# A routed-expert and time-mix block on one core: a reordered norm head, logit groups of five and three steps, and three row additions moved behind gathers

## Time and profile before

| | |
|---|---|
| Times of three runs, us | 472.74, 472.84, 476.43 |
| Profiled execution, us | 478.51 |
| Its span, us | 476.8 |
| TensorE's granted clock, mean | 0.975 |
| Busy: TensorE, VectorE, ScalarE, GpSimd | 94%, 77%, 50%, 48% |
| Moved by DMA | 77.24 MB |

### The profile page before, as it was taken

How to read it: one execution, slowest core, us unless ns; L and a number is a source line. 1 busy time by engine, 2 the same in 40 slices (tenths; PEclk the granted TensorE clock), 3 DMA queues, 4 the chain that set the end, 5 groups by cost and what they waited for, 6 DMA issues and landing times.

```text
span 476.8 us, 8300 instructions
## 1 busy us (share of the span) xinstructions
PE 445.9 (94%) x2529; PEld 372.7 (78%) x2529; DVE 365.6 (77%) x680; ACT 240.2 (50%) x394; POOL 230.8 (48%) x224
## 2 busy tenths in 40 slices
PE   0897997988999999999999899999999999999997
PEld 0562465877888888888878778888898989898987
DVE  5986596968787898688776589996868787877863
ACT  2784744497586685958565633332414132423131
POOL 5244617616658685679846286742342516070000
PEclk9998758999999999999999999999999999999999
DMA  7999813335764665443463692725343444432001
GB/s 254 393 348 280 218 24 97 93 132 164 268 234 167 214 215 178 121 155 100 144 180 132 240 332 87 242 88 160 121 145 122 127 149 132 154 108 71 24 22 45
DMA packets 45858, 77.24 MB, mean 162 GB/s; under 512 B 5908, under 2 KB 32252, under 8 KB 45820
## 3 DMA queue, kind: packets, MB, share of 16 engines
q1 hardware_dynamic: 37212, 55.83, 33.5%
q0 software_dynamic: 8240, 20.88, 16.6%
q10 hardware_dynamic: 368, 0.04, 0.1%
HBM read 48.52 MB, written 28.21 MB: 161 GB/s over the span
## 4 chain that ended last, share of the span: by engine, by line
PE 69%; DVE 12%; POOL 6%; issue 6%; ACT 4%; DMA 2%; SPq 0%; DVEq 0%; POOLq 0%; ACTq 0%
PE ps_g L1068 13%; PE ps_y L1068 7%; PE ps_w L1528 5%; PE ps_w L1530 5%; PE ps_w L1529 5%; PE ps_w L1595 5%; PE ps_w L1594 5%; PE ps_w L1593 5%; PE ps_G L590 3%; POOL xg L991 3%; PE ps_x L1062 2%; PE ps_h L1088 2%; PE ps_T L578 2%; DMA xT<-x 1%; PE ps_v L1529 1%
## 5 line engine op out<-in xcount | busy, mean ns | idle before, releaser
L991 POOL DMA_INDIRECT xg<-xn_rows,tile_tok x71 | 71.6, 1008 | 32.4 <-issue 17.9
L1504 POOL DMA_INDIRECT yg<-expert_rows,rows x64 | 67.4, 1054 | 23.6 <-issue 17.1
L1068 PE MATMUL ps_g<-w_hi,x_hi 128*128 x142 | 56.6, 398 | 1.8 <-DVE x_lo L1223 1.8
L1068 PE MATMUL ps_g<-w_hi,x_lo 128*128 x142 | 57.0, 401 | 0.0
L1068 PE MATMUL ps_g<-w_lo,x_hi 128*128 x142 | 56.7, 399 | 0.0
L1635 ACT ACTIVATE sact<-ps_w,vec_b 128x512 f32<-128x512 f32 x32 | 22.0, 687 | 58.6 <-PE ps_w L1530 58.6
L1528 PE MATMUL ps_w<-col_hi,s_hi 128*128 128x512 f32 x128 | 50.5, 394 | 0.4 <-DVE shid L1746 0.4
L1530 PE MATMUL ps_w<-col_hi,s_lo 128*128 128x512 f32 x128 | 50.2, 392 | 0.0
L1529 PE MATMUL ps_w<-col_lo,s_hi 128*128 128x512 f32 x128 | 50.2, 392 | 0.0
L1068 PE MATMUL ps_y<-w_hi,h_hi 128*128 x142 | 43.0, 303 | 1.3 <-DVE h_lo L1239 1.3
L1232 DVE TENSOR_TENSOR hid<-ps_g,act 128x512 f32<-128x512 f32 (+1 forms) x36 | 23.7, 658 | 24.4 <-ACT act L1144 24.4
(11 more groups left out here) (245 smaller groups left out, 1276.9 us busy)
## 6 DMA issues: line engine op xcount, KB each, us to landing
expert_rows<-y SPq DMA_DIRECT2D x35, 256.0 KB, 2.2
w_lo<-w_all SPq DMA_DIRECT2D x16, 384.0 KB, 9.1
table<-mix_tables SPq DMA_DIRECT2D x8, 768.0 KB, 6.2
xT<-x SPq DMA_DIRECT2D x16, 256.0 KB, 5.8
xn_rows<-xn SPq DMA_DIRECT2D x16, 256.0 KB, 7.7
xn_columns<-xT SPq DMA_DIRECT2D x8, 512.0 KB, 3.8
col<-xn_columns SPq DMA_DIRECT2D x8, 512.0 KB, 5.0
res<-x SPq DMA_DIRECT2D x16, 256.0 KB, 3.1
```

Of the source, the lines that this page charges most:

```text
L991: pool.indirect_dma_start(out=xg[b][:, t, :], out_offset=None, in_=xn_d[:, :], in_offset=bass.IndirectOffsetOnAxis(ap=tile_tok[:, first_ti ...
L1068: mm = nc.tensor.matmul(out, x[:, k, :], w[:, ds(e, 1), k, cols].rearrange("p o n -> p (o n)"), start=(k == 0 and n == 0), stop=(last and ...
L1504: pool.indirect_dma_start(out=yg[a.buf(2)][:, k, q, :], out_offset=None, in_=y_d[:, :], in_offset=bass.IndirectOffsetOnAxis(ap=picked[a.bu ...
```

## The change

The groups of steps become 0 to 4 and 5 to 7, with strips of 16 partitions; a fifth copy of the bias is loaded. The first two steps of the head are written out in a new order on ScalarE, TensorE and VectorE. TensorE makes all four `less` pieces ahead of the count. VectorE's reciprocal and product of the scores move behind `tile_tok`. GpSimd's `less_first` for pieces 13, 14 and 15 move out of `route` and stand behind the gathers of units 1, 2 and 3.

```diff
-        GROUPS = [(0, 4), (4, NSTEP)]
-        ROWS = P // 4
+        GROUPS = [(0, 5), (5, NSTEP)]
+        ROWS = P // 8
...
-        EARLY = NSTEP // 2
+        EARLY = GROUPS[0][1]
...
-            for i in range(MADE, E * KC):
+            for i in range(MADE, HIGH):
                 less_first(pool, i)
...
-                    act.wait_ge(s_small, 112)
+                    act.wait_ge(s_small, 16 * (EARLY + 3))
...
-            for j in range(4):
+            for j in range(EARLY):
                 act.dma_start(gb[j * ROWS:j * ROWS + E, :], ...)
...
             root(At(0, 0, NSTEP))
-            for i in range(NSTEP):
+            norm(At(0, 0, NSTEP))
+            act.wait_ge(s_const, 8)
+            (ones, before, minus)
+            turned(At(0, 0, NSTEP))
+            root(At(0, 1, NSTEP))
+            norm(At(0, 1, NSTEP))
+            root(At(0, 2, NSTEP))
+            turned(At(0, 1, NSTEP))
+            for i in range(2, NSTEP):
                 if i + 1 < NSTEP:
                     root(At(0, i + 1, NSTEP))
                 norm(At(0, i, NSTEP))
-                if i == 0:
-                    (s_const, ones, before, minus)
-                if i > 0:
+                if i > 2:
                     turned(At(0, i - 1, NSTEP))
-                if i == 1:
+                if i == 3:
                     (lane_b)
-                if i == 5:
+                if i == 6:
                     (first_r)
...
-            for i in range(NSTEP + 2):
+            turn(At(0, 0, NSTEP))
+            pe.wait_ge(s_small, 16 * (EARLY + 3))
+            gate(At(0, 0, NSTEP))
+            turn(At(0, 1, NSTEP))
+            gate(At(0, 1, NSTEP))
+            turn(At(0, 2, NSTEP))
+            for i in range(3, NSTEP + 2):
                 (turn i, gate i - 1, back i - 2)
...
-            for i in range(2):
+            for i in range(MADE):
                 less(i)
             pe.wait_ge(s_upto, 1)
             (ps_total, ps_place)
-            for i in range(2, MADE):
-                less(i)
             for i in range(4):
                 rest(pe, i)
...
+            (memsets of xn, moved here from constants)
             measure(At(0, 0, NSTEP))
             constants()
-            for i in range(NSTEP):
+            norm(At(0, 0, NSTEP))
+            measure(At(0, 1, NSTEP))
+            more_constants()
+            norm(At(0, 1, NSTEP))
+            measure(At(0, 2, NSTEP))
+            for i in range(2, NSTEP):
                 if i + 1 < NSTEP:
                     measure(At(0, i + 1, NSTEP))
                 norm(At(0, i, NSTEP))
...
+            take(0)
...
                 dve.wait_ge(s_exp, 1)
-                own.link(nc.vector.tensor_reduce(red[:], score[:], AX_X, ALU.add))
+                own.mark(nc.vector.tensor_reduce(red[:], score[:], AX_X, ALU.add))
+
+            def scaled():
                 own.link(nc.vector.reciprocal(gates[:, 0, :], red[:]))
                 (score times gates)
...
             (tile_tok)
+            scaled()
...
             for a in range(AHEAD):
                 gather(a)
+                if 0 < a <= E * KC - HIGH:
+                    less_first(pool, HIGH + a - 1)
```

More of the change, by code:

```diff
@@ L530, in scalar @@
             root(At(0, 0, NSTEP))
-            for i in range(NSTEP):
+            norm(At(0, 0, NSTEP))
+            act.wait_ge(s_const, 8)
+            nc.scalar.activation(ones[:], ones_f[:], ACT.Copy)
+            nc.scalar.activation(before[:], before_f[:], ACT.Copy, scale=-1.0)
+            nc.scalar.activation(minus[:], ident[:], ACT.Copy, scale=-1.0)
+            turned(At(0, 0, NSTEP))
[4 more added lines that the diff above has]
+            for i in range(2, NSTEP):
                 if i + 1 < NSTEP:
@@ L604, in tensor @@
             pe.wait_ge(s_const, 1)
-            for i in range(NSTEP + 2):
+            turn(At(0, 0, NSTEP))
[5 more added lines that the diff above has]
+            for i in range(3, NSTEP + 2):
                 if i < NSTEP:
                     turn(At(0, i, NSTEP))
-                if i == 1:
-                    pe.wait_ge(s_small, 112)
-                if 0 < i <= NSTEP:
+                if i <= NSTEP:
                     gate(At(0, i - 1, NSTEP))
-                if i > 1:
-                    back(At(0, i - 2, NSTEP))
+                back(At(0, i - 2, NSTEP))
             def less(i):
@@ L654, in constants @@
                 dve.wait_ge(s_const, 6)
-                for b in range(NN):
-                    nc.vector.memset(xn[b][:, :, C:C + 1], 1.0)
                 nc.vector.tensor_copy(row[:], row_i[:])
@@ L711, in take @@
                 ).then_inc(s_Lc, 1)
+            for b in range(NN):
+                nc.vector.memset(xn[b][:, :, C:C + 1], 1.0)
             measure(At(0, 0, NSTEP))
             constants()
-            for i in range(NSTEP):
+            norm(At(0, 0, NSTEP))
[4 more added lines that the diff above has]
+            for i in range(2, NSTEP):
                 if i + 1 < NSTEP:
@@ L758, in share @@
                 dve.wait_ge(s_exp, 1)
-                own.link(nc.vector.tensor_reduce(red[:], score[:], AX_X, ALU.add))
+                own.mark(nc.vector.tensor_reduce(red[:], score[:], AX_X, ALU.add))
+            def scaled():
                 own.link(nc.vector.reciprocal(gates[:, 0, :], red[:]))
-                own.mark(nc.vector.tensor_tensor(score[:], score[:],
+                own.link(nc.vector.tensor_tensor(score[:], score[:],
                                                  gates[:, 0, :][:, :, None].broadcast_to([P, NT, E]), ALU.mult))
@@ L836, in route @@
         return sync, gpsimd, tensor, scalar, vector, (s_tok, s_xout, s_terms, s_Tout, (s_wlo, s_both, BOTH),
-                                                   (HIGH, LOW), (split_hi, split_lo, store_columns))
+                                                   (HIGH, LOW), (split_hi, split_lo, store_columns, less_first))
 def run_experts(nc, kept, placed, xn_d, y_d, y, y_stored, firsts1, coef_stored, tab_d, vec_tf, vec_td, ident, tile_tok, tile_exp,
@@ L854, in run_experts @@
         s_tok, s_xout, s_terms, s_Tout, (s_wlo, s_both, BOTH), (HIGH, LOW), route_parts = placed
-        split_hi, split_lo, store_columns = route_parts
+        split_hi, split_lo, store_columns, less_first = route_parts
         raw_vr, col0 = vr[0], col[0]
```

## The result

The changed kernel takes 484.3 us (median; 483.6 to 484.82), beside 474.63 for the kernel before on the same chip (472.74 to 478.53). The ratio is 1.0151, with a 95% interval of 1.01 to 1.0202. It is slower, with the whole interval above 1. The four times of the kernel before spread over 5.8 us and those of the changed kernel over 1.2, so the quotient of the two medians, 1.0204, is no better guide than the ratio. Profiled execution against profiled execution, 478.51 became 484.82: +6.3, and the spans (476.8 and 483.1) say the same.

The account below looks back on a forecast made before the run. The prediction saw TensorE with 69% of the chain, nearly all of it from the experts on; +3.9 - 6.1 + 9.9 = +7.7 us on the median 472.84 gave 480.5, own range 478.5 to 483.4, widened to 476.2 to 485.5.

Parts of the forecast that it names:

- Head, +3.9: Start to last bias: work queued behind ScalarE's wait for the small loads makes the last bias 3.9 us later.
- Rival 1: Head: the small loads do not bind it, so its cost falls away; 476.6 us, chance 0.12.
- Logits to tokens, -6.1: Last logits to tokens: slots start 0.6 us sooner and VectorE's one-hot wait of 5.48 goes, 6.1 us saved.
- Rival 3: Four corrections: TensorE enters them at the lower clock and they double, +5.8 us; 486.3 at most, chance 0.10.
- Tokens to experts, +9.9: Tokens to unit one's products: ScalarE's cut of piece 12 waits for addition 13; 19.8 us against 9.88.
- Rival 2: Cut of piece 12: ScalarE's wait for addition 13 is covered, price -9.9 us; 470.6 us, chance 0.07.
- Sum, +7.7: Whole kernel: the three terms, 3.9 - 6.1 + 9.9, make it 7.7 us slower.
- The base: Whole kernel: the difference was put on the median of 472.84 us, though the profiled execution took 478.51.
- Its cuts hide there: Unit one's products: addition 15 lands by 19.3 to 22.6 us after the tokens, before they end at 24.4.

Follow-up runs that it names:

- e3: The changed kernel with the two small loads issued right behind the first step of x: 479.53 us, ratio 1.0053.
- e5: The changed kernel with corrections 2 and 3 put back behind the count: 488.69 us, ratio 1.0198.
- e6: The kernel before with one edit alone, all four corrections ahead of the count: 473.61 us, ratio 0.9899.
- e2: The changed kernel with addition 13 back in the route, only those of pieces 14 and 15 behind the gathers: 479.34 us, ratio 1.0033.
- e1: The changed kernel with all twelve additions back in the route: 474.93 us, ratio 0.9969.
- e4: The changed kernel with only additions 14 and 15 behind the gathers and the small loads early: 474.46 us, ratio 0.9931.
- e7: e4 with ScalarE's cuts of pieces 14 and 15 moved behind unit three's rows: 474.2 us, ratio 0.9903.
- e9: The changed kernel with all twelve additions back in the route and the small loads early: 475.07 us, ratio 0.9962.
- e10: The changed kernel with additions 12 to 15 behind gathers one to four, their cuts later, and the small loads early: 474.77 us, ratio 0.9955.
- e8: The kernel before run once more, unchanged, to compare its short and long executions: 478.18 us.
- e11: e6 with VectorE paused ahead of the third one-hot round until additions 12 and 13 have landed: 475.3 us in a single execution.

## Why the prediction was right, and where it was off

*Head, +3.9: measured +4.0.* ScalarE waits for `vec_td`, as the prediction said, and the last bias stands at 42.50 (42.4 predicted). e3 shows the cause by removing it. Rival 1 is out. The size fits better than the path. The sum ran through VectorE's steps and ScalarE's norm 7 (37.8 predicted, it ends at 37.35). But TensorE works without a break from 29.62 and turns that step only at 38.15, and its first logits took 3.78 where the sum's later ones take 1.72. That both paths end within 0.8 us of each other is luck, of which the +4.0 has its share.

*Logits to tokens, -6.1: measured -6.0.* The slots start 5.78 after the copy (5.7 predicted), and the 5.48 us wait is gone. e5 and e6 show from both sides that the place of corrections 2 and 3 does it; what part the lower clock had in it stays open. Rival 3, the lower clock in the corrections, did not come: the granted clock was 1.00 from 44 to 52, and the slots are on time.

*Tokens to experts, +9.9: measured +9.8.* Addition 13 starts 5.05 after the tokens (5.03 predicted) and has landed 4.8 later (5.0 taken). From x_lo of unit zero (80.03) to unit one it takes 5.70, with 4.86 + 0.8 predicted. e2 shows that ScalarE's wait for the addition is the step: without it unit one is back at 9.78 after the tokens. Rival 2 is out. The fit of the Trainium skill (DMA: Bandwidth & Descriptors, "Anatomy of one DMA — SWDGE (gpsimd) path"), by which an addition would take 2.6 us as an estimate, isn't what the runs show: the shortest of the twelve here took 4.6, as the view of line L382 in the changed kernel has it,

```profile
DMA to landing us min/median/max: 4.6/7.4/8.7
```

and the measurement decides.

*Sum, +7.7: +7.8 at unit one's start, +6.3 at the end.* The term that was mis-sized is TensorE's clock. The prediction charged 0.8 for unit zero's products at the lower level after the idle stretch, and that happened (2.92). But it left unit one's twelve at their old 4.61, though the earlier trace rows showed that these had run at 0.57. They ran at 1.00 and gave 1.55 back.

*The base.* The sum was put on a median of three runs, 472.84, two of which lie below all 31 runs of that kernel beside e1 to e4 (473.04 to 479.58, median 478.16). The profiled execution, on which all the rows rest, took 478.51, and 6.3 on that is a ratio of 1.0132, inside the interval measured. So the forecast of 480.5 was low by the base's 5.7, of which the return at unit one hid 1.4. The prediction named the difference of 5.7 and chose the wrong side of it. The measured 484.3 lies above the forecast's own range, 478.5 to 483.4. It lies inside 485.5 only because the range was stretched there for rival 3, which did not come: the sizes of the steps were right, but it is luck that the range holds the time.

*Its cuts hide there.* That sentence on pieces 14 and 15 holds only as long as the first wait delays unit one. With the first wait gone, e2 and e4 show 6.2 to 6.3 us of ScalarE's waiting for them.

*Where the rest of the gain went.* The order of the corrections alone gives 5.2 (e6): unit one starts 3.4 us sooner there (74.56 against 77.94), and its products take 3.06 instead of 4.61. The new head gives 1.1 to 1.7 more at the last bias once the small loads come early (37.42 in e7 and 36.82 in e9, against 38.49). Yet e7 and e9, which have both, are at 0.9903 and 0.9962 no faster than e6 at 0.9899. In their profiled executions the held addition takes the second gain back, in e7 by ScalarE's wait and in e9 by the late gather: unit one starts 13.4 and 14.7 us after the tokens, where it took 9.88, and so at 74.63 and 75.12, no sooner than in e6. e10, which avoids it, pays with a late row of its own. The lowest ratios are those of e6 and e7, both 1% under the kernel before; their intervals overlap with that of e4. What remains open is why single executions of one kernel lie 5 us and more apart (e1 from 473.8 to 478.8, the kernel before from 473.0 to 479.6), beyond what e8 says of the clock.

## What to carry to other kernels

A transfer that is moved behind a late event takes with it every wait on its semaphore: look whether other transfers count on that semaphore, and what stands behind the wait on the waiting engine; two additions on one semaphore cost 14.6 us of idling here. When an order is tightened so that a wait disappears (5.5 us here), ask what used that pause; here GpSimd issued additions in it, and without it one of them was held in four of the profiled kernels. And put a sum on the execution that its rows come from before carrying it to a median of a few runs.

## What the runs showed of the hardware

An addition issued by GpSimd takes 1.5 to 1.75 us there in most rows, but 7.7 to 9.4 in e1, e6, e7 and e9, where it starts among VectorE's one-hot rounds running without a break. In all four it ends 0.11 to 0.12 us after exp_f ends (62.14 against 62.03 in e6), and with a pause of 5.1 us in the rounds it doesn't occur (e11). Each of these is one profiled execution. Not every addition in the rounds is held: the one at 55.83 in the changed kernel took 1.75. The place alone does not decide: e4 and e7 have the same instructions up to there, and addition 13, issued 4.13 and 4.11 us after the rounds began, took 1.75 in one and 8.07 in the other. Which is held stays open.

The Trainium skill (SBUF — State Buffer, "Who interferes with whom") says that GpSimd and VectorE share a pair of SBUF ports, and that a VectorE instruction with two SBUF inputs contends with a GpSimd instruction that reads SBUF. The one-hot operations and tile_no have two inputs in SBUF, and the addition's indices lie there, so the held additions agree with that part. But the page has `tensor_reduce` never contend on this chip, and reports that neither it nor `tensor_tensor` stalled DMAs; here the hold lasts through a run of `tensor_tensor`, and it outlasts tile_no by the whole of exp_f, a reduction, in all four runs. The measurement decides, but that the ports are the cause is not shown. Either the reduction holds GpSimd too, or some 0.8 us of the addition's own work follows once tile_no lets go; no run here tells these apart.
